# A three-layer decoder on one core: x1's row scales ahead of the projections, M steps spread out, a new order on all engines

## The reference, cut to what matters

```
x  = layernorm(x + attn(x))                    # x: 16 batches of 256 rows, 512 columns
x  = layernorm(x + xattn(x, ctx))              # ctx: 16 x 256 x 128
out = layernorm(x + moe(x))                    # 64 experts, top 6, capacity 128, plus a shared one
attn:  for 3 heads  Q,K,V = x @ W.T ; softmax over the QUERY axis ; mean over heads ; @ fc_w.T + fc_b
xattn: 16 heads of 32, causal, softmax over keys: q = x @ Wq.T, k,v = ctx @ Wkv.T, out @ Wout.T
```

## Time and profile before

| | us |
|---|---|
| median of three runs | 2077.9 (2069.2 to 2090.6) |
| the profiled execution | 2056.9, its span 2055.2 |
| PE busy | 1993.3, 97% of the span |
| DVE busy | 1645.9, 80% |
| ACT, POOL busy | 1028.8, 722.5 |
| mean granted clock of TensorE | 0.993 |

### The profile page before, as it was taken

The page is one execution under the profiler, slowest core; times in us unless marked ns, Lnnn a source line. Parts: engine busy times, 40 slices in busy tenths (PEclk is TensorE's granted clock), DMA queues, the critical chain, the costliest instruction groups (busy, mean ns, idle before and its releaser), DMA issues.

```text
span 2055.2 us, 46172 instructions
## 1 busy us (share of the span) xinstructions
PE 1993.3 (97%) x16976; PEld 1228.0 (60%) x16976; DVE 1645.9 (80%) x3682; ACT 1028.8 (50%) x1569; POOL 722.5 (35%) x709
## 2 busy tenths in 40 slices
PE   8999999999999999999999987999999999998998
PEld 3666666676676666666667654455555555554553
DVE  5557988888888898898888888858888888877867
ACT  5425434444453553544445354536565665555545
POOL 1003223323323322332332321535555454544533
PEclk9999999999999999999999998999999999999999
DMA  6801011011011001101101122489999999998948
GB/s 227 79 24 45 13 54 54 0 54 54 10 44 54 23 30 54 54 0 54 54 4 50 43 89 78 152 230 280 292 297 288 299 296 293 287 278 270 284 87 327
DMA packets 134324, 267.24 MB, mean 130 GB/s; under 512 B 32699, under 2 KB 42939, under 8 KB 134236
## 3 DMA queue, kind: packets, MB, share of 16 engines
q1 hardware_dynamic: 110108, 226.06, 33.9%
q0 software_dynamic: 24128, 40.01, 10.0%
HBM read 208.67 MB, written 57.42 MB: 129 GB/s over the span
## 4 chain that ended last, share of the span: by engine, by line
PE 78%; DVE 11%; DMA 6%; issue 3%; ACT 1%; POOL 1%; DVEq 0%; POOLq 0%; ACTq 0%
PE ring L915 34%; PE moe_bank L1705 20%; PE ring L975 6%; DVE quad L1294 6%; DMA expert_sums<-tion_then_expert_weights,scatter_index 4%; PE moe_bank L1774 4%; PE fold L483 3%; PE quad L1030 2%; DVE maxima L1294 2%; PE ring L1047 2%; PE ring L982 1%; PE moe_bank L1740 1%; PE ring L1055 1%; DMA expert_sums<-tion_then_expert_weights 1%; PE moe_bank L1752 1%
## 5 line engine op out<-in xcount | busy, mean ns | idle before, releaser
L178 POOL DMA_INDIRECT slot_table<-table_records,slot_of_choice x204 | 202.9, 994 | 482.3 <-PE ring L915 327.7
L915 PE MATMUL ring<-xT_split,tion_then_expert_weights 128*128 128x256 f16 x2304 | 267.2, 273 | 0.0
L915 PE MATMUL ring<-tion_then_expert_weights,xT_split 128*128 128x512 f16 x1152 | 259.9, 379 | 0.0
L915 PEld LDWEIGHTS ring<-xT_split,tion_then_expert_weights 128*128 128x128 f16 x2304 | 221.9, 98 | 36.8 <-issue 7.9
L1154 ACT ACTIVATE scratch<-ring 128x512 f16<-128x512 f32 x224 | 130.5, 595 | 199.8 <-PE ring L915 199.5
L885 POOL TENSOR_SCALAR_AFFINE_SELECT scratch<-scratch 128x1024 f32<-128x1024 f32 x64 | 70.3, 1099 | 379.1 <-ACT scratch L1174 376.3
L1654 POOL DMA_INDIRECT expert_sums<-tion_then_expert_weights,scatter_index x64 | 125.7, 1965 | 193.2 <-DMA expert_sums<-tion_then_expert_weights,scatter_index 58.6
L915 PEld LDWEIGHTS ring<-tion_then_expert_weights,xT_split 128*128 128x128 f16 x1152 | 109.0, 98 | 131.9 <-issue 7.9
L1294 DVE CUSTOM_DVE_ANT_0 quad<-quad,causal_penalty 128x128 f32<-128x128 f32 (+1 forms) x512 | 164.8, 394 | 13.8 <-PE quad L1013 10.7
L1255 DVE SCALAR_TENSOR_TENSOR scratch<-ring,scratch 128x512 f16<-128x512 f32 x192 | 129.1, 684 | 44.3 <-ACT scratch L1154 44.3
L1705 PE MATMUL moe_bank<-w_down_split,hidden_T_split 128*128 128x512 f16 x576 | 136.2, 382 | 5.8 <-DVE hidden_T_split L1921 5.8
(11 more groups left out here) (246 smaller groups left out, 4015.7 us busy)
## 6 DMA issues: line engine op xcount, KB each, us to landing
gate_up_landing<-in_w_gate SPq DMA_DIRECT2D x43, 704.0 KB, 5.7
gate_up_landing<-in_w_up SPq DMA_DIRECT2D x43, 704.0 KB, 5.9
scratch<-in_w_down SPq DMA_DIRECT2D x43, 512.0 KB, 4.8
scratch<-in_w_gate SPq DMA_DIRECT2D x21, 704.0 KB, 5.6
scratch<-in_w_up SPq DMA_DIRECT2D x21, 704.0 KB, 5.8
tion_then_expert_weights<-in_w_down SPq DMA_DIRECT2D x21, 512.0 KB, 4.9
scratch<-in_w_down SPq DMA_DIRECT2D x43, 192.0 KB, 6.3
xT_in<-in_xT SPq DMA_DIRECT2D x16, 512.0 KB, 4.4
```

The costliest lines, as they stand in the source:

```text
L178: pool.indirect_dma_start(self.dram, bass.IndirectOffsetOnAxis(ap=self.slot[:, tb, c:c + 1], axis=0), self.record[:, tb, c, :], None, boun ...
L915: last = pe.matmul(out_, left(a, c), right(b, c), start=(n == 0 and not onto), stop=(n == 3 * chunks - 1))
```

## The change

1. LN is two steps: LN(1,0) for x1 after O(1,0), LN(2,0) for x2 after OUT(1,0), with a semaphore each (`scaled1`, `scaled2`). NX1 waits for the first only.
2. In the loop T, K, C and Q of the cross attention come right after V(0,0) and Y(0,0), and the four M stand among V(0,1), Y, TX, S, R, C. TX, R, RC come later than before. P(0,0) stands behind RM and RS on DVE, CT behind ST(0,0) on PE. The lists of bodies 16 and 17 are reordered as well (K, T before C; RS last in the tail; SU(0,0) behind LN).
3. The maxima are written as f16, and transposed through an f16 identity (`ident16`, made once by POOL) into f16 PSUM.
4. In body 16 x1 is written to `x1_last`, in the columns of the attention weights `ws`, which are unused by then; elsewhere NX1 waits for the OUT(1,0) that still reads x1.
5. Scatters wait for other steps; `BEFORE_EXPERTS` is 16 instead of 14.

```diff
 PE_BODY = [
-    ("Y", 0, 0), ("C", 0, 0), ("V", 0, 0), ("V", 0, 1), ("TX", 0, 0), ("TX", 1, 0), ("Y", 0, 1), ("T", 0, 0),
-    ("T", 1, 0), ("C", 1, 0), ("K", 0, 0), ("R", 0, 0), ("Q", 0, 0), ("K", 1, 0), ("Q", 1, 0), ("S", 0, 0),
-    ("S", 0, 1), ("M", 0, 0), ("Y", 1, 0), ("M", 1, 0), ("V", 1, 0), ("M", 2, 0), ("Y", 1, 1), ("M", 3, 0),
-    ("V", 1, 1), ("MT", 0, 0), ("MT", 1, 0), ("CT", 0, 0), ("ST", 0, 0), ("S", 1, 0), ("S", 1, 1),
...
+    ("V", 0, 0), ("Y", 0, 0), ("T", 0, 0), ("T", 1, 0), ("K", 0, 0), ("K", 1, 0), ("C", 0, 0), ("Q", 0, 0),
+    ("Q", 1, 0), ("TX", 0, 0), ("V", 0, 1), ("M", 0, 0), ("Y", 0, 1), ("TX", 1, 0), ("M", 1, 0), ("S", 0, 0),
+    ("S", 0, 1), ("R", 0, 0), ("M", 2, 0), ("Y", 1, 0), ("C", 1, 0), ("V", 1, 0), ("M", 3, 0), ("Y", 1, 1),
+    ("V", 1, 1), ("MT", 0, 0), ("MT", 1, 0), ("S", 1, 0), ("ST", 0, 0), ("CT", 0, 0), ("S", 1, 1), ("Y", 2, 0),
+    ("ST", 1, 0), ("Y", 2, 1), ("ST", 2, 0), ("AV", 0, 0), ("V", 2, 0), ("S", 2, 0), ("S", 2, 1), ("AV", 1, 0),
+    ("ST", 3, 0), ("V", 2, 1), ("AV", 2, 0), ("O", 0, 0), ("AV", 3, 0), ("O", 1, 0), ("OUT", 0, 0),
+    ("OUT", 1, 0),
 DVE_BODY = [
...
+    ("V", 0, 0), ("Y", 0, 0), ("T", 0, 0), ("T", 1, 0), ("C", 0, 0), ("K", 0, 0), ("Q", 0, 0), ("K", 1, 0),
+    ("TX", 0, 0), ("Q", 1, 0), ("V", 0, 1), ("M", 0, 0), ("Y", 0, 1), ("TX", 1, 0), ("M", 1, 0), ("S", 0, 0),
+    ("S", 0, 1), ("R", 0, 0), ("S1", 0, 0), ("M", 2, 0), ("Y", 1, 0), ("C", 1, 0), ("RC", 0, 0), ("M", 3, 0),
+    ("V", 1, 0), ("Y", 1, 1), ("MT", 0, 0), ("V", 1, 1), ("MT", 1, 0), ("S2", 0, 0), ("CT", 0, 0), ("S", 1, 0),
+    ("S", 1, 1), ("S1", 1, 0), ("RM", 0, 0), ("RS", 0, 0), ("P", 0, 0), ("S2", 1, 0), ("Y", 2, 0), ("Y", 2, 1),
+    ("P", 1, 0), ("AV", 0, 0), ("S", 2, 0), ("V", 2, 0), ("S", 2, 1), ("P", 2, 0), ("S1", 2, 0), ("OM", 0, 0),
+    ("AV", 1, 0), ("V", 2, 1), ("S2", 2, 0), ("P", 3, 0), ("OM", 1, 0), ("AV", 2, 0), ("AV", 3, 0),
+    ("OM", 2, 0), ("OM", 3, 0), ("O", 0, 0), ("O", 1, 0), ("LN", 1, 0), ("OUT", 0, 0), ("OUT", 1, 0),
+    ("LN", 2, 0),
 DVE_TAIL = [
+    ("SU", 1, 0), ("TX", 0, 0), ("SH", 0, 0), ("TX", 1, 0), ("SU", 2, 0), ("R", 0, 0), ("RC", 0, 0),
+    ("SH", 1, 0), ("SH", 2, 0), ("CT", 0, 0), ("SU", 3, 0), ("SH", 3, 0), ("RM", 0, 0), ("SU", 4, 0),
+    ("SH", 4, 0), ("RS", 0, 0),
...
-LINKS_A, LINKS_B, LINKS_C, LINKS_LN = 6, 4, 12, 14
+LINKS_A, LINKS_B, LINKS_C = 20, 18, 12
...
+    x1_last = ws[:, :, :, :, :].rearrange("p a h t n -> p (a h t n)").bitcast(F32)[:, 0:NB * E]\
+        .rearrange("p (t n) -> p t n", t=NB)
-    mx = mem.sb("maxima", [P, NB, P], F32)
+    mx = mem.sb("maxima", [P, NB, P], F16)
...
-                    last = pe.transpose(o[:, 0:P], mx[:, g, :], ident[:, :])
+                    last = pe.transpose(o[:, 0:P // 2].bitcast(F16), mx[:, g, :], w["ident16"][:, :])
...
                 elif name == "NX1":
-                    act.wait_ge(scaled, b.i)
+                    act.wait_ge(scaled1, b.n(1, 0, 0, 0))
+                    to = x1_last if b.is_(B) else x1
+                    if not (b.is_(1) or b.is_(B)):
+                        act.wait_ge(free, b.last_freed("OUT", 1, 0))
...
+                elif name == "LN" and g == 1:
+                    dve.wait_ge(free, b.freed("O", 1, 0))
+                    row_scales(0, pre, scaled1)
                 elif name == "LN":
-                    rows = []
-                    if b.a:
-                        dve.wait_ge(free, b.freed("O", 1, 0))
-                        rows += [(t, pre[:, t, :]) for t in range(NB)]
-                    if b.b:
-                        dve.wait_ge(free, b.freed("OUT", 1, 0))
-                        rows += [(NB + t, pre2[:, t, :]) for t in range(NB)]
-                    row_scales(rows)
+                    dve.wait_ge(free, b.freed("OUT", 1, 0))
+                    row_scales(NB, pre2, scaled2)
...
-BEFORE_EXPERTS = 14
+BEFORE_EXPERTS = 16
```

More of the change, by code:

```diff
@@ L244, in build @@
                 pick=mem.sb("pick_head", [P, EC, P], F16),
-                ones=mem.sb("ones", [P, P], F16),
+                ones=mem.sb("ones", [P, P], F16), ident16=mem.sb("ident_16", [P, P], F16),
                 before=mem.sb("earlier_tokens", [P, P], F16),
@@ L393, in on_gpsimd @@
         pool.memset(w["ones"][:, :], 1.0).then_inc(const, 1)
+        pool.wait_ge(const, 1)
+        pool.tensor_copy(w["ident16"][:, :], ident[:, :]).then_inc(const, 1)
         then_wait(pool.memset(w["before"][:, :], 0.0))
@@ L408, in on_gpsimd @@
         pool.tensor_copy(w["empty"][:, :, 0], empty_id[:, :]).then_inc(const, 1)
-        pool.wait_ge(const, 9)
+        pool.wait_ge(const, 10)
         pool.wait_ge(w["xT_loaded"], 16)
@@ L488, in prepare @@
     return Stage(on_sync, on_gpsimd, on_scalar, on_vector, on_tensor, dict(
-        split=(low, len(items)), rows=(rows_done, 3), constants=(const, 9), folded=(fold_low, len(folds))))
+        split=(low, len(items)), rows=(rows_done, 3), constants=(const, 10), folded=(fold_low, len(folds))))
 PE_BODY = [
[6 rows of a table removed]
-    ("O", 1, 0), ("OUT", 0, 0), ("OUT", 1, 0),
[6 rows of a table added]
+    ("OUT", 1, 0),
 ]
@@ L538 @@
 SCATTER_BEHIND = [
-    (-1, ("V", 2, 1)), (-1, ("O", 0, 0)), (-1, ("O", 1, 0)), (-1, ("OUT", 1, 0)), (0, ("C", 0, 0)), (0, ("V", 0, 0)),
-    (0, ("V", 0, 1)), (0, ("Y", 0, 1)), (0, ("Q", 0, 0)), (0, ("S", 0, 1)), (0, ("Y", 1, 0)), (0, ("V", 1, 0)),
+    (-1, ("AV", 3, 0)), (-1, ("AV", 3, 0)), (-1, ("O", 1, 0)), (-1, ("OUT", 0, 0)), (-1, ("OUT", 1, 0)), (0, ("V", 0, 0)),
+    (0, ("K", 1, 0)), (0, ("Q", 0, 0)), (0, ("Q", 1, 0)), (0, ("TX", 0, 0)), (0, ("C", 1, 0)), (0, ("Y", 1, 1)),
 ]
 SCATTER_BEHIND_LAST = [
-    (-1, ("V", 2, 1)), (-1, ("O", 0, 0)), (-1, ("O", 1, 0)), (-1, ("OUT", 0, 0)), (-1, ("OUT", 1, 0)), (0, ("K", 1, 0)),
+    (-1, ("AV", 3, 0)), (-1, ("AV", 3, 0)), (-1, ("O", 1, 0)), (-1, ("OUT", 0, 0)), (-1, ("OUT", 1, 0)), (0, ("K", 1, 0)),
     (0, ("T", 1, 0)), (0, ("Q", 0, 0)), (0, ("Q", 1, 0)), (0, ("TX", 1, 0)), (0, ("R", 0, 0)), (0, ("C", 1, 0)),
@@ L577 @@
 PE_TAIL = [
[L578 removed]
+    ("SU", 2, 0), ("SU", 3, 0), ("TX", 0, 0), ("TX", 1, 0), ("SG", 4, 0), ("R", 0, 0), ("SU", 4, 0),
+    ("CT", 0, 0),
 ]
 ACT_TAIL = [
[L581 to L582 removed]
+    ("NX2", 0, 0), ("SH", 0, 0), ("TX", 0, 0), ("SH", 1, 0), ("TX", 1, 0), ("SH", 2, 0), ("SG", 4, 0),
+    ("RM", 0, 0), ("SH", 3, 0), ("SH", 4, 0),
 ]
 DVE_TAIL = [
[L585 to L586 removed]
+    ("SU", 1, 0), ("TX", 0, 0), ("SH", 0, 0), ("TX", 1, 0), ("SU", 2, 0), ("R", 0, 0), ("RC", 0, 0),
+    ("SH", 1, 0), ("SH", 2, 0), ("CT", 0, 0), ("SU", 3, 0), ("SH", 3, 0), ("RM", 0, 0), ("SU", 4, 0),
+    ("SH", 4, 0), ("RS", 0, 0),
 ]
@@ L698, in attend @@
     rec_used = mem.sem("records_used")
-    scaled = mem.sem("attention_row_scales")
+    scaled1, scaled2 = mem.sem("x1_row_scales"), mem.sem("x2_row_scales")
     gu, x2t, hs = loads.gate_up, loads.x2t, loads.hidden
@@ L733, in own @@
                     (self.a if s[0] in A_STEPS else self.c if s[0] in C_STEPS else
-                     self.a or self.b if s[0] == "LN" else self.b)]
+                     self.a if s == ("LN", 1, 0) else self.b)]
         def is_(self, i):
@@ L945, in emit @@
                         pe.wait_ge(folds["folded"][0], folds["folded"][1] - RING + 1 + b.ring.index(s))
-                if s == ("Y", 0, 0):
+                if b.a and s == [r for r in b.ring if r[0] in ("Y", "V")][0]:
                     pe.wait_ge(xT_split, b.n(1, 0, 0, 1))
@@ L1136, in emit @@
                 elif name == "NX1":
-                    act.wait_ge(scaled, b.i)
+                    act.wait_ge(scaled1, b.n(1, 0, 0, 0))
+                    to = x1_last if b.is_(B) else x1
+                    if not (b.is_(1) or b.is_(B)):
+                        act.wait_ge(free, b.last_freed("OUT", 1, 0))
                     for t in range(NB):
-                        last = act.activation(x1[:, t, :], pre[:, t, :], ACT.Identity,
+                        last = act.activation(to[:, t, :], pre[:, t, :], ACT.Identity,
                                               scale=rstd[:, t:t + 1], bias=shift[:, t:t + 1])
@@ L1142, in emit @@
                 elif name == "NX2":
-                    act.wait_ge(scaled, b.i)
+                    act.wait_ge(scaled2, b.n(0, 1, 0, 0))
                     act.wait_ge(x2_stored, b.n(0, 0, 32, 1))
@@ L1209, in link, with row_scales @@
                 links[0] += 1
-                dve.wait_ge(dve_step, done_before(b.i, LINKS_A, LINKS_B, LINKS_C) + b.i * LINKS_LN + (1 + links[0]))
-            def row_scales(rows):
+                dve.wait_ge(dve_step, done_before(b.i, LINKS_A, LINKS_B, LINKS_C) + (1 + links[0]))
+            def row_scales(n0, src2, scaled):
+                n1 = n0 + NB
+                rows = [(n0 + t, src2[:, t, :]) for t in range(NB)]
                 for n, src in rows:
@@ L1220, in row_scales @@
                 link(last)
-                n0, n1 = rows[0][0], rows[-1][0] + 1
```

(5 more changed lines are left out.)

10 lines of the change are left out of this document (2 added, 8 removed), and 57 rows, old and new, of tables (ACT_BODY, ACT_LAST, DVE_BODY, DVE_FIRST).

## The result

The changed kernel takes **2169.0 us** (median of four runs, 2161.9 to 2194.5) where the kernel before takes 2074.8: ratio 1.043, 95% interval 1.035 to 1.051. My 2081 and my range to 2104 were both too low. Ratios here are of fast executions alone (none more than 1.5% above the fastest of its kernel), so they can differ a little from the quotient of two medians. Its profiled execution has a span of 2160.2 us, 105.0 more than before.

What follows compares the result with a forecast made beforehand. PE's queue was taken to set the time nearly everywhere. Loop +8.4, hand-over -3.4 and entry -1.6 gave +3.4 us on the profiled 2056.9, carried over to a forecast of 2081 us; range 2054 to 2104.

Steps and rivals of the forecast that it cites:

- (3): Split norm in the loop: second chain adds 2.6 us plus 0.3 of DVE work; PE loses 0.3 us a body at K(0,0).
- Step 1: Spread M steps in the loop: PE loses about 2.0 us a body at M(1,0), S(0,0), MT, S(1,0), against 1.8 before.
- Step 2: P(0,0) behind RM and RS on DVE in the loop: AV(0,0) waits 0.6 to 0.7 us where nothing waited.
- the 0.2 us slots: Second norm chain: small DVE instructions start 0.20 apart, making 2.6 us; the skill's page would give 2.1, 0.3 a body less.
- Step 4: MT transposes in f16 on PE in the loop: 0.25 us a body gained.
- The slower rival: Loop, P(0,0) to LN of x1: DVE becomes the bound with 0.3 slack; +1.9 us a body, 2100 us; chance 0.18.
- the forecast of no change: Whole kernel: the time differs by less than 1% (21 us) from the kernel before; chance 0.69.
- The hand-over: Last two bodies: Q in body 16 starts at 1233.8 instead of 1237.2, 3.4 us gained, idle pieces of 2.9 and 1.6 left.
- the entry: Before the experts' first gathered rows: two more PE jobs, 6.3 us of work, fill idle time of 0.9 and 1.3; 1.6 us gained.

Runs made afterwards that it cites:

- moved by 45: Changed kernel with 45 empty DVE instructions at the start of DVE's program, so its loop stands 45 places further on: 2118.9 us, ratio 1.020.
- the split version with the hint: Changed kernel with the old orders in the loop's body, the split row scales kept, and hint_back_edge on DVE's loop: 2055.3 us, ratio 0.998.
- The shortened chains: Changed kernel without x1's three Newton steps and two of x2's three, DVE's loop cut to 283 instructions: 2087.5 us, ratio 1.014.
- aligned: Changed kernel without empty instructions, the head of DVE's loop laid on the start of a 128-instruction block: 2122.0 us, ratio 1.027.
- with the hint: Changed kernel with hint_back_edge=True on DVE's loop: ratio 1.034.

## Why the prediction was wrong

The account of the loop's 116.4 us: **56.6 instruction fetches** (after against moved by 45), 27 the clash with POOL, 34 other waits of the new order, -1.5 the split and the f16 transposes (the split version with the hint against the kernel before). The 34 are what is left over: no run takes them apart. The prediction had 8.4 for the whole loop.

*What it left out.* The failed step is the cost of splitting the norm, (3), which was put at 0.3 us a body. It counted the second chain's time on DVE and not its instructions as code; that term was put at nothing and came to 56.6 us, 4.0 a body. That the number of instructions counts was applied to DVE's time alone: 27 more instructions in the loop, and 13 ahead of it, brought the loop into a fourth block. No rival had it. What the profile offered was the 33 packets of the instruction queue; it did not show that this is a loop on DVE that 13 more instructions make 3.4% slower.

*Step 1, the M stage.* Place right, size too small: M(1,0) waits 0.54 (0.8 expected), MT's bank 0.24, S(1,0) 0.46, S(0,0) 0.20: 1.44 a body in waits, where the kernel before shows 0.54 and 0.29. That is 0.6 more; the step had 0.2 more.

*Step 2, AV(0,0) behind RM and RS.* Wrong: AV(0,0) has no wait. The waits come later, at AV(1), O(0,0), AV(3) and OUT(0,0).

*Step 3.* The second chain is as long as said, and DVE's wait before OUT is gone. K(0,0) waits 0.61 once the fetches are away (version moved by 45), not 0.3:
```profile
438.06 1.48 PE L920 MATMUL ring<-ctx_split,wkv_split 128*128 128x256 f16 x12 [0.61 <-DVE scratch L1266]
```
The shortened chains say what the length is worth: 15 small instructions, 3 us of DVE a body (0.20 each in the trace, not the 0.27 of the expectation), less made the loop 12.7 us shorter (1183.6 to 1170.9), 0.9 a body, and the waits of O and AV(3) stayed. So my weighing of the 0.2 us slots touched a term of that size at most.

*Step 4.* Nothing measurable.

*The slower rival* had the right place, from P(0,0) to the row scales, and the right sort of price: 1.9 a body against the 2.5 that the trace shows there (AV(1) 0.25, O(0,0) 1.05, AV(3) 0.76, OUT(0,0) 0.48). Its reason was half right. The slack of 0.3 us was gone at once, as it said, but through S2, at 0.8 a pair in my sum and 1.72 and 2.42 in the trace. I had taken DVE's durations from the earlier trace rows as if they belonged to the instruction; they belong to it and to what POOL does beside it. I gave this rival 0.18 and its sum ended at 2100. Without the fetches the kernel is at 1.020, 1.027 and 1.034 of the one before (moved, aligned, with the hint), beyond that, so even then the forecast of no change would have failed.

*The hand-over and the entry.* Q came 2.7 us sooner (3.4 expected), with idle pieces of 1.07, 3.03 and 1.50 (2.9 and 1.6 expected). It was given back: the whole stretch is 2.4 us longer at a clock of 0.86. The entry holds: X(1) 4.1 us later after the last CT with 6.3 us more work done, so 2.2 gained against 1.6, and the idle time under 1.5. Behind it the span is 14.1 us shorter: the two jobs' 6.3, and a stall of 5.8 that the run of before happened to have; 2.0 are open.

## What to carry to other kernels

Before adding instructions to a loop, count all of them on that engine, and look at the instruction queue's packets in the profile: a loop that fits owes it partly to where it starts, and an edit of code *ahead* of it can cost as much as one within. For the 313 instructions here a fixed place or the hint at the loop's head took that chance out. And when a step is moved on DVE, price it by what POOL does at the new time: beside a mask or a split of x, S2 took two to three times as long here, and P(3) 2.22 us instead of 1.75.

No version here is measurably faster than the kernel before; the split with the old order and the hint (0.998, 0.994 to 1.001) is its equal.

## What the runs showed of the hardware

- DVE's loop: 98 packets, and from 56 us (changed kernel against moved) to 76 us (shortened roots) more in the loop, once it reaches into a fourth block of 128 instructions; with the hint 33 packets, at four blocks too.
- PE's loop has some 1566 matmuls and weight loads a body (10963 and 10962 in fourteen), and the instruction queue that the changes in DVE's code leave alone, which I take for PE's, has 55 packets in every run: no sign that PE's loop is fetched again. That agrees with the 128 KB that the Trainium skill (Advanced Engine Details and Errata, ISA Cache) gives for TensorE.
- DVE's low half of 2 times 256 columns from two SBUF operands: 0.87 us alone, 1.72 beside a mask of POOL, 2.41 to 2.88 beside its split of x; a reciprocal from PSUM keeps 1.75 beside either.
- Twelve runs of the split version with the hint lie between 2041.8 and 2071.5 us. Its traced run, at the upper end (2070.9), has five stalls of about 4 us behind DVE's `hidden_T_split` in the expert stage, and the trace of the kernel after has none; differences of one such trace behind the loop say little.
